# Two waited fills behind every fourth indirect transfer in place of one unwaited fill behind each

## The chip, the cores and the metric

The kernel runs on one core of a Trainium2 chip. A core has five engines that run side by side: TensorE (PE in the profile), VectorE (DVE), ScalarE (ACT), GpSimd (POOL) and SyncE (SP). They meet at semaphores. The metric is the device time of one execution in microseconds. The kernel before took 2920.82 us, the median of three runs from 2917.95 to 2922.92 us.

## What is computed

Two layers of a network on a graph of 3125 nodes with 256 features, and 50,000 edges. Each layer adds a sum over edges, an attention term and the output of experts, with a normalisation between the parts.

```python
# layer 0: messages over edges
support = x @ weight
out = segment_sum(support[col] * edge_weight[:, None], row) + bias
# layer 0: eight private experts, two chosen per node, and a shared one
routed = sum(gate[e] * (gelu(x @ W1p[e] + b1p[e]) @ W2p[e] + b2p[e])); out = shared + routed
# layer 1: messages over edges, weighted by exp(score) per head
messages = h_fwd[src] * direction[:, 0:1] + h_rev[src] * direction[:, 1:2]
# layer 1: a graph-attention router over 32768 edges picks two of four experts
```

Everything that is read or written by an index (rows of edges, of nodes, of experts' slots) goes through indirect transfers.

## The kernel before

Nodes stand in 25 tiles of 128 rows. Edges are first put in the order of their target: each of the 391 columns of 128 edge records is scattered to its place in a table in HBM. Then a stage reads the sorted table back, gathers the source row of each edge (128 rows a transfer), and TensorE sums 128 edges into a tile of nodes by a product with a one-hot matrix that VectorE makes.

All indirect transfers are issued by GpSimd, from one list of instructions in program order:

- `scatter_records` (L840): 391 columns of layer 0's edges (`slots_gnn<-rec_gnn`), later 391 of layer 1's in two parts of 48 and 343.
- `gather_rows` (L1232): 416 gathers of `support` rows for `sum0_stage`. A ring of 16 tiles (`FLIGHT`) is refilled, and before every fourth gather (`HALF` is 4) GpSimd waits for `used`, which TensorE sets when a half of eight tiles has been multiplied.
- `send_nodes0` (L1700): 50 scatters of normed rows to the experts' slots; `fetch_outputs0` (L1721): 50 gathers of the experts' output.
- `gather_messages` (L2373): 440 gathers for layer 1's sum (`sum1_stage`).
- `norm3_table_g_stage` (L2707): 25 scatters; `attend_stage` (L2947, L2959): 256 gathers of `table_g` rows in eleven cuts of about 24, each behind a wait for VectorE, then 25 gathers.

That makes 391 + 416 + 48 + 50 + 343 + 50 + 440 + 25 + 256 + 25 = 2044 indirect transfers. In the scatters and in `gather_messages` GpSimd waits before every fourth transfer until the four that were issued sixteen earlier have landed.

Behind each of the 2044 transfers the helper `breathe` (L816 to L819) issues a fill of one bf16 element per partition: `pool.memset(c.idle[:, c.breaths:c.breaths + 1], 0.0)`. Nothing reads the element. It signals no semaphore and nobody waits for it. So that no two fills write the same element, `c.idle` is 512 wide (`BREATHS`) and in some stages is laid over other tiles that are not in use (`idle_sum0`, `before`, `head32`); the profile shows it as `idle`, `idle_sum`, `before` or `head` at L818.

Beside the transfers, in the order of the program: norm, attention and sort work of layer 0 runs beside the first scatter; the router and the first three chunks of the shared expert run beside the sends and the second scatter; then the private experts (L1843, L1855) run with GpSimd waiting for their output.

Of the kernel before, what the change touches and what calls it, by code (L numbers as in the profile page):

```python
# [21 lines left out]
BF16 = mybir.dt.bfloat16  # L22
# [5 lines left out]
P = 128  # L28
# [8 lines left out]
HALF = RING // 2  # L37
# [29 lines left out]
class Core:  # L67
# [16 lines left out]
    def clear_spent(self):  # L84

        self.nc.all_engine_barrier()
        self.nc.clear_and_free_semaphores(self.spent)
        self.nc.all_engine_barrier()
        self.spent = []
        self.breaths = 0  # L90


def meet(eng, met, n):
# [15 lines left out]
def stage_setup(c, ctx):  # L109
# [13 lines left out]
    c.part = c.sb(ctx, "part", [P, 1])  # L123
    c.head32 = c.sb(ctx, "head32", [P, P])
    c.head64 = c.sb(ctx, "head64", [P, P])
    c.idle = c.sb(ctx, "idle", [P, BREATHS], BF16)
    c.breaths = 0
    c.rows_loaded = c.sem(ctx, "node_rows_loaded")
    const_sem = c.sem(ctx, "constants_made")
    c.tail_zeroed = c.sem(ctx, "tail_zeroed")  # L130
# [682 lines left out]
        ch.then(dve.tensor_copy(self.e.idx[:], self.bank[:, 0:self.e.per]))  # L813


def breathe(c, pool):  # L816

    pool.memset(c.idle[:, c.breaths:c.breaths + 1], 0.0)  # L818
    c.breaths += 1  # L819


def scatter_records(c, block, ctx, e, begin=0, end=None):
# [861 lines left out]
PLACED_A_ROUND = 5  # L1684
SHARED_FIRST = 3
SCATTERED_FIRST = 48
BREATHS = 512


def send_nodes0(c, block, ctx):  # L1690
# [1151 lines left out]
def attend_stage(c, block, ctx, er, e1, y, b2, b2_in, met_n):  # L2842
# [91 lines left out]
    @block.gpsimd  # L2934
    def _(pool):
        pool.wait_ge(met, 4 * (met_n - 1))
        pool.sem_inc(turns, 1)
        for k, (lo, hi) in enumerate(cuts):
            if k >= 2:
                pool.wait_ge(taken, k - 1)  # L2940
                pool.sem_inc(turns, 1)
            for j in range(lo, hi):
                h, turn = j % FLIGHT // HALF, j // FLIGHT
                if j % HALF == 0 and turn:
                    pool.wait_ge(rows_in[h], 16 * HALF * turn)
                    pool.sem_inc(turns, 1)
                pool.indirect_dma_start(rows[:, k % 2, j - lo, :], None, c.table_g,  # L2947
                                        bass.IndirectOffsetOnAxis(er.idx[:, j:j + 1], 0)).then_inc(rows_in[h], 16)
                breathe(c, pool)
        for h in range(2):  # L2950
            pool.wait_ge(stored[h], 16 * len(cuts[h::2]))
            pool.sem_inc(turns, 1)
        c.idle, c.breaths = c.before[:].bitcast(BF16), 0
        for t in range(T):
            h, turn = t % RING // HALF, t // RING
            if t % HALF == 0 and turn:
                pool.wait_ge(ends_in[h], 16 * HALF * turn)
                pool.sem_inc(turns, 1)
            pool.indirect_dma_start(at_end[:, t, :], None, er.states,  # L2959
                                    bass.IndirectOffsetOnAxis(er.end_at[:, t:t + 1], 0)).then_inc(ends_in[h], 16)  # L2960
            breathe(c, pool)
# [465 lines left out]
def build(nc, a, out, upto=4):  # L3427


    c = Core(nc, a, out)  # L3430
    c.upto = upto
    with ExitStack() as top:
        top.enter_context(nc.allow_non_contiguous_dma("small strided rows"))
        c.kept.append(top)
        stage_setup(c, top)
        c.support = nc.dram_tensor("support", [NP, D], F32, kind="Internal").ap()

# [6 lines left out]
        with ExitStack() as l0:  # L3444
# [5 lines left out]
            with ExitStack() as s, nc.Block() as block:  # L3450
# [7 lines left out]
                with ExitStack() as st:  # L3458
                    sort_stage(c, block, st, er, 4)
                load_slots(c, block, l0, e0)  # L3460
                kept_idle = c.idle
                c.idle, c.breaths = c.sb(s, "idle_sum0", [P, BREATHS], BF16), 0
                wait_for_clears = clear_slots0(c, block, s, er)
                sum0_stage(c, block, s, e0, Placing(c, s, er, c.bank[:, 7, :]), Ranking(c, s, e1, c.bank[:, 6, :]))
                block.scalar(wait_for_clears)
            c.idle = kept_idle
            c.clear_spent()
        if c.upto >= 2:
            with ExitStack() as l1:
# [31 lines left out]
                if c.upto >= 3:  # L3501
# [9 lines left out]
                    with nc.Block() as block:  # L3511
                        with ExitStack() as s:
# [6 lines left out]
                            for stage in (lambda st, m: sum1_stage(c, block, st, e1, mix, m),  # L3519
                                          lambda st, m: norm3_table_g_stage(c, block, st, er, e1, m)):  # L3520
                                m += 1
                                with ExitStack() as st:
                                    stage(st, m)
                        c.idle, c.breaths = c.head32[:].bitcast(BF16), 0
                        y = c.sb(l1, "experts_out", [P, EXPERTS1 - 1, T, D])
                        b2 = c.sb(l1, "b2_1", [P, EXPERTS1, D])
                        b2_in = c.sem(l1, "b2_loaded_1")
# [57 lines left out]
```

## Time and profile before

| | us |
|---|---|
| median of three runs | 2920.82 |
| lowest and highest | 2917.95, 2922.92 |
| span of the profiled execution | 4223.8 |
| POOL busy in the profiled execution | 2236.3 (53%) |
| PE busy | 2387.8 (57%) |
| DVE busy | 1680.7 (40%) |
| ACT busy | 1177.6 (28%) |

The profile shows one execution, made with the profiler on. Its span is 4223.8 us, and the kernel's own median is 2920.82 us: the profiled execution is longer by 1303 us, a factor of 1.446. A stretch of the profile can therefore not be taken as the same stretch of a timed run. In the rows, "busy" leaves out semaphore and register instructions, and "idle before" is the time that an engine stood still before an instruction, with what ended it; "issue" means that nothing that the profile shows was waited for.

### The profile page before, as it was taken

To read this page: it belongs to the slowest core of one execution; us is meant where nothing else is said; L and a number is where in the kernel's file an instruction comes from. 1 tells how busy PE (TensorE), PEld (TensorE's weight loads), DVE (VectorE), ACT (ScalarE), POOL (GpSimd) and SP (SyncE) were. 2 spreads that over 40 slices of the span, in tenths; PEclk is the share of its full clock that TensorE was granted. 3 is DMA by queue.
4 is the path that set the end of the run, shared out by engine and by line. 5 is a ranking of instruction groups with operands and counts; after the bars stand their busy time and mean duration, and the time that the engine had idled before them with its cause. 6 is when DMAs were issued, how large, how long until landed. Compare 5 with 4: busy or idle time off the path is not lost. (4 is left out here: it accounts for less than half of the span.)

```text
span 4223.8 us, 36587 instructions
## 1 busy us (share of the span) xinstructions
PE 2387.8 (57%) x9996; PEld 1783.9 (42%) x9997; DVE 1680.7 (40%) x4678; ACT 1177.6 (28%) x3151; POOL 2236.3 (53%) x4104
## 2 busy tenths in 40 slices
PE   0034245445555536443259999736776675677784
PEld 0021134323443335112148887624455454455563
DVE  6510049955577731000000001435777674212225
ACT  0000013534444411000012221235785452222232
POOL 5777740057777755777730001367677735445441
PEclk9985555567777756555579999867997785778787
DMA  1000000043333312000036664122222231010101
GB/s 45 2 18 14 14 3 3 1 178 89 91 88 89 87 32 84 2 2 2 2 106 195 195 190 155 56 73 47 44 46 46 48 21 38 8 21 14 21 13 33
DMA packets 173406, 233.47 MB, mean 55 GB/s; under 512 B 59819, under 2 KB 136622, under 8 KB 172206
## 3 DMA queue, kind: packets, MB, share of 16 engines
q0 software_dynamic: 73664, 103.00, 11.2%
q1 hardware_dynamic: 96888, 118.21, 8.9%
q10 hardware_dynamic: 2678, 10.29, 0.6%
q8 instruction: 65, 1.06, 0.1%
q14 instruction: 111, 0.91, 0.1%
HBM read 192.31 MB, written 39.04 MB: 55 GB/s over the span
## 5 line engine op out<-in xcount | busy, mean ns | idle before, releaser
L840 POOL DMA_INDIRECT slots_gnn<-rec_gnn,slot_row_gnn x782 | 754.5, 965 | 299.6 <-issue 237.7
L1232 POOL DMA_INDIRECT rows_gnn<-support,xT x416 | 402.0, 966 | 437.1 <-DMA xT<-slots_gnn 276.9
L2373 POOL DMA_INDIRECT arena<-table,rec_gnn x440 | 443.8, 1009 | 195.2 <-issue 90.8
L2947 POOL DMA_INDIRECT source_rows<-table_g,source_router x256 | 242.0, 945 | 252.5 <-DVE weighted_rows L3191 158.9
L1277 PE MATMUL banks<-rows_gnn,one_hot 128*128 128x256 f32 x832 | 267.9, 483 | 184.1 <-issue 161.9
L3071 PE MATMUL banks<-xT,w 128*128 128x256 f32 (+1 forms) x832 | 232.0, 411 | 159.3 <-issue 148.2
L1721 POOL DMA_INDIRECT expert_row_ring<-slot_y,slot_from x50 | 48.0, 961 | 510.7 <-SPq L1822 457.3
L1277 PEld LDWEIGHTS banks<-rows_gnn,one_hot 128*128 128x128 f32 x832 | 197.2, 248 | 247.0 <-issue 205.6
L2472 PE MATMUL banks<-weighted,one_hot 128*128 128x260 f32 x880 | 273.4, 464 | 37.9 <-issue 22.1
L3071 PEld LDWEIGHTS banks<-xT,w 128*128 128x128 f32 x832 | 169.2, 209 | 210.6 <-issue 178.8
L1843 PE MATMUL banks<-slot_xT,w_private 128*128 128x256 f32 x1024 | 229.6, 383 | 33.5 <-ACT hidden_private L1885 31.5
L2472 PEld LDWEIGHTS banks<-weighted,one_hot 128*128 128x128 f32 x880 | 191.0, 227 | 97.7 <-issue 62.1
L1885 ACT ACTIVATE hidden_private<-banks,b_private 128x256 f32<-128x256 f32 x256 | 107.3, 470 | 447.0 <-PE banks L1843 417.7
L1855 PE MATMUL banks<-w_private,hidden_private 128*128 128x256 f32 x1024 | 226.1, 379 | 0.0
L1843 PEld LDWEIGHTS banks<-slot_xT,w_private 128*128 128x128 f32 x1024 | 196.7, 192 | 61.4 <-ACT hidden_private L1885 31.7
L796 ACT ACTIVATE lane_one_hot<-lanes_apart,packed_router,packed_minus_router 128x128 bf16<-128x128 bf16 x512 | 203.9, 480 | 2.1
L1855 PEld LDWEIGHTS banks<-w_private,hidden_private 128*128 128x128 f32 x1024 | 192.2, 190 | 24.9
L1497 DVE TENSOR_TENSOR shared_out<-banks,b 128x512 f32<-128x512 f32 (+1 forms) x8 | 5.3, 658 | 493.3 <-remote 492.9
L1631 PE MATMUL banks<-w,hidden_shared 128*128 128x256 f32 x240 | 121.0, 566 | 132.6 <-issue 128.4
L1310 DVE TENSOR_TENSOR x<-banks,x 128x256 f32 x416 | 176.0, 423 | 45.6 <-issue 0.8
L3084 PE MATMUL banks<-w,hidden 128*128 128x256 f32 x668 | 174.6, 407 | 27.0 <-issue 26.8
L790 ACT ACTIVATE lanes_apart<-iota,slot_lane_router 128x128 bf16<-128x128 bf16 x256 | 81.2, 388 | 384.6 <-remote 271.8
(562 smaller groups left out, 4667.0 us busy)
## 6 DMA issues: line engine op xcount, KB each, us to landing
w_private<-in_w1p SPq DMA_DIRECT2D x32, 1024.0 KB
w_private<-in_w2p SPq DMA_DIRECT2D x32, 1024.0 KB
slots_gnn<-rec_gnn,slot_row_gnn POOLq DMA_INDIRECT x782
slot_x<-zero_rows ACTq DMA_DIRECT2D x8, 1024.0 KB
slot_rows<-slot_x SPq DMA_DIRECT2D x32, 256.0 KB
slot_y<-slot_out SPq DMA_DIRECT2D x32, 256.0 KB, 2.2
arena<-table,rec_gnn POOLq DMA_INDIRECT x440
rows_gnn<-support,xT POOLq DMA_INDIRECT x416
```

The lines of the kernel that those rows point to most:

```text
L796: op = act.activation(self.lane_hot[:, b % 2, k, q, :], self.apart[:, b % 2, k, :], ACT.Relu, bias=e.value[:, q, j:j + 1], scale=e.minus[: ...
L840: pool.indirect_dma_start(e.slots, bass.IndirectOffsetOnAxis(e.rows[:, j:j + 1], 0), e.rec[:, j, :], None)\
L1232: pool.indirect_dma_start(e.rows_in[:, k, :], None, table, bass.IndirectOffsetOnAxis(row, 0))\
L1277: mm = pe.matmul(bank_of(k // per), hot[:, k, :], e.rows_in[:, row, :], start=k % per == 0, stop=k % per == per - 1)
L1310: dve.tensor_tensor(x, bank_of(g), x, ALU.add).then_inc(added, 1)
L1843: mm = pe.matmul(hidden_room(f), w1[:, b, k, f * P:(f + 1) * P], xT[:, b, k, :], start=k == 0, stop=k == KD - 1)
L1855: mm = pe.matmul(c.bank[:, 6 + b, j * D:(j + 1) * D], hid[:, b, f, j * P:(j + 1) * P], w2[:, b, f, :], start=f == 0, stop=f == FC - 1)
L2373: pool.indirect_dma_start(c.raw[:, t % RAW_RING, :], None, c.table1, bass.IndirectOffsetOnAxis(row, 0))\
L2472: mm = pe.matmul(c.bank[:, k // per, 0:AGG], hot[:, k, :], val[:, k, :, :].rearrange("p h f -> p (h f)"), start=k % per == 0, stop=k % per ...
L2947: pool.indirect_dma_start(rows[:, k % 2, j - lo, :], None, c.table_g, bass.IndirectOffsetOnAxis(er.idx[:, j:j + 1], 0)).then_inc(rows_in[h ...
L3071: mm = pe.matmul(hidden_room(n, f, (hi - lo) * P), w1[:, x % 2, k, f * P:(f + 1) * P], c.xT[:, k, lo * P:hi * P], start=k == 0, stop=k == ...
L3084: mm = pe.matmul(out_room(n, t - lo), hid(n, f)[:, (t - lo) * P:(t - lo + 1) * P], w2[:, x % 2, f, :], start=f == 0, stop=f == FC - 1)
```

## The change

`breathe` no longer fills behind each transfer. It counts, and at every fourth transfer it calls a new helper, `rest`, which fills one element twice. Each fill signals a semaphore, and GpSimd waits for it before it goes on. The counter runs through the whole program and isn't set back. The wide `idle` tile, the tiles laid over it and the constant `BREATHS` go; one element and a semaphore `rested` come.

```diff
--- before.py
+++ after.py
@@ -87,7 +87,6 @@
         self.nc.clear_and_free_semaphores(self.spent)
         self.nc.all_engine_barrier()
         self.spent = []
-        self.breaths = 0
 
 
 def meet(eng, met, n):
@@ -123,8 +122,9 @@
     c.part = c.sb(ctx, "part", [P, 1])
     c.head32 = c.sb(ctx, "head32", [P, P])
     c.head64 = c.sb(ctx, "head64", [P, P])
-    c.idle = c.sb(ctx, "idle", [P, BREATHS], BF16)
-    c.breaths = 0
+    c.idle = c.sb(ctx, "idle", [P, 1], BF16)
+    c.rested = c.sem(ctx, "rested")
+    c.breaths = c.rests = 0
     c.rows_loaded = c.sem(ctx, "node_rows_loaded")
     const_sem = c.sem(ctx, "constants_made")
     c.tail_zeroed = c.sem(ctx, "tail_zeroed")
@@ -813,10 +813,19 @@
         ch.then(dve.tensor_copy(self.e.idx[:], self.bank[:, 0:self.e.per]))
 
 
+def rest(c, pool):
+
+    for _ in range(2):
+        pool.memset(c.idle[:], 0.0).then_inc(c.rested, 1)
+        c.rests += 1
+        pool.wait_ge(c.rested, c.rests)
+
+
 def breathe(c, pool):
 
-    pool.memset(c.idle[:, c.breaths:c.breaths + 1], 0.0)
     c.breaths += 1
+    if c.breaths % HALF == 0:
+        rest(c, pool)
 
 
 def scatter_records(c, block, ctx, e, begin=0, end=None):
@@ -1684,7 +1693,6 @@
 PLACED_A_ROUND = 5
 SHARED_FIRST = 3
 SCATTERED_FIRST = 48
-BREATHS = 512
 
 
 def send_nodes0(c, block, ctx):
@@ -2950,7 +2958,6 @@
         for h in range(2):
             pool.wait_ge(stored[h], 16 * len(cuts[h::2]))
             pool.sem_inc(turns, 1)
-        c.idle, c.breaths = c.before[:].bitcast(BF16), 0
         for t in range(T):
             h, turn = t % RING // HALF, t // RING
             if t % HALF == 0 and turn:
@@ -3458,12 +3465,9 @@
                 with ExitStack() as st:
                     sort_stage(c, block, st, er, 4)
                 load_slots(c, block, l0, e0)
-                kept_idle = c.idle
-                c.idle, c.breaths = c.sb(s, "idle_sum0", [P, BREATHS], BF16), 0
                 wait_for_clears = clear_slots0(c, block, s, er)
                 sum0_stage(c, block, s, e0, Placing(c, s, er, c.bank[:, 7, :]), Ranking(c, s, e1, c.bank[:, 6, :]))
                 block.scalar(wait_for_clears)
-            c.idle = kept_idle
             c.clear_spent()
         if c.upto >= 2:
             with ExitStack() as l1:
@@ -3521,7 +3525,6 @@
                                 m += 1
                                 with ExitStack() as st:
                                     stage(st, m)
-                        c.idle, c.breaths = c.head32[:].bitcast(BF16), 0
                         y = c.sb(l1, "experts_out", [P, EXPERTS1 - 1, T, D])
                         b2 = c.sb(l1, "b2_1", [P, EXPERTS1, D])
                         b2_in = c.sem(l1, "b2_loaded_1")
```

In GpSimd's list this turns 2044 fills without a wait into 1022 fills with one. In the first scatter (L840 before, L849 after), from the transfer that waits for the landing of an earlier four (`records_moved`), before:

```order
L840 DMA slots_gnn0<-rec_gnn0,slot_row_gnn0 53639x4 [waits records_moved_gnn0_0_0]
L818 MEMSET idle 128x1
L840 DMA slots_gnn0<-rec_gnn0,slot_row_gnn0 53639x4
L818 MEMSET idle 128x1
L840 DMA slots_gnn0<-rec_gnn0,slot_row_gnn0 53639x4
L818 MEMSET idle 128x1
L840 DMA slots_gnn0<-rec_gnn0,slot_row_gnn0 53639x4
L818 MEMSET idle 128x1
L840 DMA slots_gnn0<-rec_gnn0,slot_row_gnn0 53639x4 [waits records_moved_gnn0_0_1]
```

and of the change:

```order
L849 DMA slots_gnn0<-rec_gnn0,slot_row_gnn0 53639x4 [waits rested,records_moved_gnn0_0_0]
L849 DMA slots_gnn0<-rec_gnn0,slot_row_gnn0 53639x4 x3
L819 MEMSET idle 128x1
L819 MEMSET idle 128x1 [waits rested]
L849 DMA slots_gnn0<-rec_gnn0,slot_row_gnn0 53639x4 [waits rested,records_moved_gnn0_0_1]
```

Four transfers stand back to back; the second fill waits for the first, and the next transfer for the second.

In the gathers of `sum0_stage` (L1232 before, L1241 after; `rows_used0` is what TensorE sets), before:

```order
L1232 DMA rows_gnn0<-support,xT 128x256 [waits rows_used0]
L818 MEMSET idle_sum0 128x1
L1232 DMA rows_gnn0<-support,xT 128x256
L818 MEMSET idle_sum0 128x1
L1232 DMA rows_gnn0<-support,xT 128x256
L818 MEMSET idle_sum0 128x1
L1232 DMA rows_gnn0<-support,xT 128x256
L818 MEMSET idle_sum0 128x1
L1232 DMA rows_gnn0<-support,xT 128x256 [waits rows_used0]
```

and of the change:

```order
L1241 DMA rows_gnn0<-support,xT 128x256 [waits rows_used0]
L819 MEMSET idle 128x1
L819 MEMSET idle 128x1 [waits rested]
L1241 DMA rows_gnn0<-support,xT 128x256 [waits rested]
L1241 DMA rows_gnn0<-support,xT 128x256 x2
L1241 DMA rows_gnn0<-support,xT 128x256 [waits rows_used0]
```

Since 391 transfers went before, the pair of fills stands here behind the gather that waits for TensorE, and not ahead of it.

## Rows read from the trace of the kernel before

**Rows 1.** The page's head: span, busy time of each engine, its slices.
```profile
span 4223.8 us, 36587 instructions
PE 2387.8 (57%) x9996; PEld 1783.9 (42%) x9997; DVE 1680.7 (40%) x4678; ACT 1177.6 (28%) x3151; POOL 2236.3 (53%) x4104
POOL 5777740057777755777730001367677735445441
```

**Rows 2.** Busy us (and instructions) of each engine in stretches; then clock, DMA share, GB/s.
```profile
core 0: us, PE busy (x) PEld busy (x) DVE busy (x) ACT busy (x) POOL busy (x), PEclk, DMA share, GB/s
38.00:594.00 556.00, 139.81 (x320) 74.11 (x321) 155.84 (x431) 28.21 (x44) 425.08 (x782) 0.76 0.05 10
594.00:870.00 276.00, 134.66 (x1464) 108.67 (x1463) 234.55 (x437) 95.01 (x194) 0.00 (x0) 0.53 0.02 6
870.00:1488.00 618.00, 332.33 (x1316) 245.08 (x1317) 401.36 (x1229) 282.02 (x768) 456.71 (x832) 0.77 0.35 105
1488.00:1684.00 196.00, 100.28 (x402) 82.73 (x401) 54.99 (x200) 22.38 (x49) 105.88 (x196) 0.63 0.19 59
1684.00:2168.00 484.00, 175.62 (x324) 88.68 (x324) 8.53 (x13) 16.74 (x42) 368.16 (x686) 0.51 0.04 8
2168.00:2624.00 456.00, 450.24 (x2136) 395.90 (x2136) 43.57 (x63) 104.75 (x250) 0.00 (x0) 0.99 0.58 182
...
2759.00:3424.00 665.00, 425.12 (x1426) 287.27 (x1427) 424.25 (x1111) 372.32 (x1174) 494.64 (x880) 0.80 0.26 49
...
3553.00:4078.00 525.00, 362.67 (x1399) 284.55 (x1401) 104.75 (x433) 120.44 (x246) 271.59 (x512) 0.78 0.11 18
```

**Rows 3.** Timeline of POOL in the first scatter: start us, us, instruction, idle before.
```profile
48.41 0.98 POOL L840 DMA_INDIRECT slots_gnn<-rec_gnn,slot_row_gnn  x1 [0.19 <-issue]
49.39 0.12 POOL L818 MEMSET idle<- 128x1 bf16 x1
49.69 0.96 POOL L840 DMA_INDIRECT slots_gnn<-rec_gnn,slot_row_gnn  x1 [0.19 <-issue]
50.65 0.12 POOL L818 MEMSET idle<- 128x1 bf16 x1
50.95 0.96 POOL L840 DMA_INDIRECT slots_gnn<-rec_gnn,slot_row_gnn  x1 [0.19 <-issue]
```

**Rows 4.** POOL's groups over the span: count | busy us, mean ns | idle before, releasers.
```profile
L1232 POOL DMA_INDIRECT rows_gnn<-support,xT x416 | 402.0, 966 | 437.1 <-DMA xT<-slots_gnn 276.9 <-remote 80.0 <-issue 60.0
L2373 POOL DMA_INDIRECT arena<-table,rec_gnn x440 | 443.8, 1009 | 195.2 <-issue 90.8 <-DMA support<-support_ring 41.1 <-PE banks L2472 35.2
L2947 POOL DMA_INDIRECT source_rows<-table_g,source_router x256 | 242.0, 945 | 252.5 <-DVE weighted_rows L3191 158.9 <-issue 93.4
L1721 POOL DMA_INDIRECT expert_row_ring<-slot_y,slot_from x50 | 48.0, 961 | 510.7 <-SPq L1822 457.3 <-DVE x L2120 46.1 <-issue 7.3
```

**Rows 5.** Timeline of POOL in the setup: an instruction that waits for POOL's own fill.
```profile
1.36 0.20 POOL L143 MEMSET ident<- 128x128 f32 x1
1.81 0.28 POOL L144 TENSOR_SCALAR_AFFINE_SELECT ident<-ident 128x128 f32<-128x128 f32 x1 [0.24 <-POOL ident L143]
```

**Rows 6.** Timeline where POOL stood in a wait: in `sum0_stage`, then in `attend_stage`.
```profile
999.65 1.11 DVE L1298 TENSOR_SCALAR one_hot<-iota,xT 128x128 f32<-128x128 f32 x4 [3.65 <-PE banks L1277]
1000.40 0.94 POOL L1232 DMA_INDIRECT rows_gnn<-support,xT  x1 [2.21 <-PE banks L1277]
...
3708.14 0.90 DVE L3191 TENSOR_TENSOR weighted_rows<-source_rows,edge_weights 128x384 f32<-128x384 f32 x1 [40.26 <-ACT edge_weights L2998]
...
3710.23 0.94 POOL L2947 DMA_INDIRECT source_rows<-table_g,source_router  x1 [20.04 <-issue]
```

**Rows 7.** Waits in the stretch 1684 to 2168 us: total us, times, longest.
```profile
DVE shared_out L1497 <- remote: 458.9, 6, 89.6
...
PEld banks L1631 <- issue: 157.9, 137, 2.6
...
PE banks L1618 <- issue: 111.9, 104, 2.4
POOL slots_gnn L840 <- issue: 109.5, 343, 2.2
PE banks L1631 <- issue: 109.0, 106, 2.2
```

## The prediction

> **What bounds the kernel now.** I read the page's head first. No engine is busy for more than 57% of the span, so the end is set by different engines in different stages; the slices of POOL show GpSimd at 7 to 8 tenths in four long stretches, broken by stretches of zero [rows 1]. The table of stretches says what each is [rows 2]. From 38 to 594 us (the first scatter), 870 to 1488 us (the gathers of `sum0_stage`), 1684 to 2168 us (the second scatter) and 2759 to 3424 us (the gathers of `sum1_stage`) POOL is busy for 74 to 76% of the time, and no other engine is above 65%. From 2168 to 2624 us PE is busy for 450 of 456 us, and POOL for none. From 3553 to 4078 us PE leads with 363 of 525.
>
> Why POOL is at 75% and still the bound shows in its timeline [rows 3]. A transfer takes 0.96 us, the fill starts where it ends and takes 0.12 us, and the next transfer starts 0.19 us after the fill, "issue" being all that it waited for. The period from start to start is 1.26 us (49.69 to 50.95), and the 0.19 us count as idle. So GpSimd has no free time in such a stretch. Where it really waits, its groups tell [rows 4]: 80 us for "remote" work in the gathers of `sum0_stage`, 41 + 35 us in those of `sum1_stage`, 159 us for VectorE in the table gathers of `attend_stage`, 46 us for VectorE in the fetches behind the experts (the 457 us before them are one wait for the experts' output).
>
> **What is removed.** The count is exact: 2044 fills without a wait. For four transfers the time between the end of one and the start of the next is 4 x (0.12 + 0.19) = 1.24 us now [rows 3].
>
> **What is added.** 511 times (2044 / 4) a pair of fills, each waited for. Take the time between transfers for a group of four after the change. Between the four transfers there are three gaps without a fill. The trace has no two transfers back to back, so the gap is bounded by 0 (the 0.19 us belong to the fill) and 0.19 us (they belong to the transfer). I take 0.19 us: it is the same before each transfer in the steady rows, and the fill itself starts with no gap at all, so the gap goes with the kind of instruction that follows. Then comes the first fill, 0.12 us. The second fill waits for the first: the nearest row is the setup's L144, which waits for POOL's own fill L143; that ends at 1.36 + 0.20 = 1.56 us and L144 starts at 1.81, 0.24 us later [rows 5]. The second fill takes another 0.12 us. Then the next transfer waits for it, and this is the term that matters. Before the change GpSimd's sequencer has the next transfer ready behind the fill; after it, the transfer can only be begun once the semaphore is there. What that costs shows where POOL stood in a wait [rows 6]. At 999.65 us VectorE and at 1000.40 us GpSimd start behind the same TensorE product: GpSimd's transfer is 0.75 us later. In `attend_stage` VectorE's product that frees the buffer ends at 3708.14 + 0.90 = 3709.04 us, and the transfer starts at 3710.23, 1.19 us later. The bounds for a restart are thus 0.24 us (if a transfer restarts as fast as L144) and 1.19 us; I take 0.75, since one semaphore alone is waited for, as at 1000.40.
>
> The group: 3 x 0.19 + 0.12 + 0.24 + 0.12 + 0.75 = 1.80 us in place of 1.24, so **+0.56 us for four transfers**, 11% of 5.04 us. With 1.19 us it is +1.00, with 0.24 us +0.05, and with the lower bound of both (0 and 0.24) -0.52 us.
>
> A rule of the notes speaks against the 0.75 us. The Trainium skill, "DMA: Bandwidth & Descriptors", section "Anatomy of one DMA — SWDGE (gpsimd) path", puts the dispatch by the sequencer at about 50 ns and the generation of descriptors at "small, variable". By it the restart would be an estimated 0.05 + 0.19 = 0.24 us and the group +0.05 us, the second rival below. The trace's 0.75 us [rows 6] does not agree with it, and the trace decides.
>
> **What queues behind the waits.** Everything behind a fill on GpSimd is the next transfer; for it wait TensorE's products in the two sums (they need the gathered rows) and, in the scatters, the reload of the sorted table, which needs all of them. By stages, in the profiled execution's time:
>
> - first scatter, 391 transfers, 98 groups: 98 x 0.56 = 55 us.
> - gathers of `sum0_stage`, 416, 104 groups: 58 us. The 80 us in which GpSimd waits for others [rows 4] can take some: what POOL loses between two such waits shortens the next. I count half, 29 us.
> - 48 scatters and 50 sends ahead of the experts, 24 groups: 14 us.
> - second scatter, 343, 86 groups: 48 us.
> - gathers of `sum1_stage`, 440, 110 groups: 62 us against 76 us of waits; half, 31 us.
> - the 25 scatters and 25 gathers at the router's ends, 12 groups: 7 us.
> - `attend_stage`'s 256 gathers (64 groups, 36 us) are hidden by its 159 us of waits for VectorE, the 50 fetches (12 groups, 7 us) by their 46 us [rows 4]. Without that cover they would cost 43 us.
>
> Sum: 55 + 29 + 14 + 48 + 31 + 7 = **184 us** of a span of 4224 us, 4.4%. The smaller `idle` tile moves no work.
>
> **From the profiled execution to the timed one.** The span is 1.446 times the median of 2920.82 us, and the trace doesn't say where the 1303 us lie. PE's stretch at 450 of 456 us cannot have lost much, so the GpSimd stretches must have. A first way is to scale: 184 / 1.446 = 127 us, which gives 3048. But in the two scatters GpSimd isn't alone in being slow. TensorE issues 324 products in 484 us there, against 2136 in 456 us in the next stretch, and between them it stands in gaps of "issue", 112 + 109 us [rows 2, 7]. Much of that is work that in a faster execution would end earlier or later than the scatter by itself, and behind the first scatter VectorE is busy for 235 of 276 us. I can't tell from the trace whether GpSimd is still the bound in the two scatters when the kernel is timed, and count half of their 103 us. That leaves 184 - 52 = 132 us, and 132 / 1.446 = **91 us: 3012 us**, 3.1% slower.
>
> **Rivals.**
>
> 1. *The restart is dearer* (1.19 us, +1.00 for a group). The row at 3710.23 speaks for it; the one at 1000.40 is closer to the case. 91 x 1.00 / 0.56 = 163 us gives 3084; with the scatters in full, 127 x 1.79 = 227 us gives 3148. It would also hold if back-to-back transfers were slower each than those with a fill between, of which the trace shows nothing.
>
> 2. *The wait is cheap or covered.* A restart at L144's 0.24 us makes +0.05 us for a group: 434 groups on the path x 0.05 / 1.446 = 15 us, 2936. If in the timed execution VectorE, TensorE and ScalarE are the bound in both sums (they are busy for 401 of 618 and 425 of 665 us already, with a POOL that is slow), next to nothing is left, and the time stays at 2921. For it: those busy shares. Against: a scatter of 98 transfers ahead of the experts and the ends of the router have no cover.
>
> 3. *It gets faster*: the 0.19 us belong to the change from a fill to a transfer. Then three of four gaps go, and the group is 0.12 + 0.24 + 0.12 + restart. It is a gain as soon as the restart is under 1.24 - 0.48 = 0.76 us; at 0.75 it is nothing, at 0.50 it is -0.26 us, and 434 x 0.26 / 1.446 = 78 us less gives 2843. In the same direction: if TensorE's "issue" gaps in the scatters [rows 7] come from GpSimd's transfers, each pause behind a fourth transfer lets TensorE go on. Against: the fill starts behind a transfer without any gap, so no gap goes with a change of kind as such.
>
> That the change doesn't do what it says is excluded by GpSimd's order: four transfers, two fills, the waits on `rested`.
>
> **How the numbers follow.** The forecast (a restart near 0.75 us, partly covered) has 0.62, and spans 2950 to 3125. Rival 1 beyond 3125 has 0.08, rival 2 has 0.17 (0.10 of it within 0.2% of 2920.82, which is about what a measurement of this kernel can tell from no change, and 0.07 slower by 2927 to 2950), rival 3 has 0.13. The likeliest is the forecast, 3012 us. The range must leave out no more than 0.2: at the upper end it cuts at 3125 and leaves out 0.08; at the lower end it takes in rival 2 whole and ends at 2915, leaving out nearly all of rival 3. Faster 0.13, same 0.10, slower 0.62 + 0.08 + 0.07 = 0.77.
>
> **What would show it.** In the changed kernel's profile, in the first scatter: three gaps of 0.19 us between transfers of 0.96 us, then two fills of 0.12 us with 0.24 us between, and 0.75 us to the next transfer; 5.6 us from the first transfer of a group to that of the next, where it is 5.05 now. A gap of 0 between transfers is rival 3, a restart of 0.24 us rival 2, one of 1.2 us rival 1. The span should be near 4224 + 184 = 4408 us; the waits for others in the gathers of both sums shorter than 80 and 76 us; the stretch of the private experts unchanged at some 456 us. The forecast is wrong if the timed execution isn't bound by GpSimd where the profiled one is, or if a transfer's own duration depends on what stands before it.

## The result: 5.1% slower, and a profile of before from another condition

| | us |
|---|---|
| kernel before, median of four runs beside it | 2919.39 (2917.41 to 2922.92) |
| change, median of four runs | 3070.11 (3061.61 to 3071.31) |
| ratio | 1.0507, 95% interval 1.0495 to 1.052 |
| span of the change's profile | 3068.5 |

The change is 151 us slower; the prediction had said 91. The head of its page:

```profile
span 3068.5 us, 35567 instructions
PE 2195.5 (72%) x9997; PEld 1686.8 (55%) x9997; DVE 1684.1 (55%) x4678; ACT 1184.5 (39%) x3151; POOL 2134.3 (70%) x3082
...
POOL 4667676667777776777777754777777772777761
```

The span is no longer than the timed run. The profile of before had 4223.8 us [rows 1], so by the two profiles the change would be 27% faster, and by the timed runs it is 5.1% slower. The two profiles can't be compared: one and the same program, the kernel before, took 2919 and 2925 us in two sessions (below: *quick*) and 4178, 4185 and 4222 us in three others (below: *slow*), each time with little spread. The profile of before belongs to the second kind, and profiling is not what makes it long, as the first experiment shows. The three slow sessions ran on three different chips (numbers 7, 6 and 4) and the second quick one on a fourth (number 0); for the first quick one and the profile of before the chip isn't on record. No chip was used twice, so nothing here tells whether a chip is slow or a time is.

The first scatter in the change, GpSimd's timeline (start us, us, instruction, idle before):

```profile
55.59 0.96 POOL L849 DMA_INDIRECT slots_gnn<-rec_gnn,slot_row_gnn  x1 [0.30 <-issue]
56.85 0.95 POOL L849 DMA_INDIRECT slots_gnn<-rec_gnn,slot_row_gnn  x1 [0.30 <-issue]
58.11 1.01 POOL L849 DMA_INDIRECT slots_gnn<-rec_gnn,slot_row_gnn  x1 [0.30 <-issue]
59.12 0.27 POOL L819 MEMSET idle<- 128x1 bf16 x2
60.21 0.96 POOL L849 DMA_INDIRECT slots_gnn<-rec_gnn,slot_row_gnn  x1 [0.82 <-POOL idle L819]
```

Two things stand here that the rows of before could not show. Between two transfers with no fill there are 0.30 us, exactly the 0.12 + 0.19 us that stood there with one [rows 3]: from start to start it is 1.26 us with and without. And behind the pair of fills it takes 0.82 us until a transfer that has a landing's wait ahead of it too. Where no such wait follows, it is 0.28 us. In the program, that place holds two things between the pair and the transfer: the wait for the landing, and an increment of the semaphore `turns` by GpSimd itself. No run separates the two. Without a waited fill ahead of them they cost nothing: in the kernel with no fill at all (below), the longest gap of this kind before a scatter is 0.3 us too. So "directly ahead of the landing's wait" means below: ahead of the wait and its increment.

### The profile page after: what moved, and what is told of

It is laid out like the page before. It is cut to its first block and busy times, and to the rows that moved or that the text cites. A ratio compares the mean times of both kernels' runs of the same rounds, so it can differ in the third digit from the quotient of the medians.

```text
span 3068.5 us, 35567 instructions
## 1 busy us (share of the span) xinstructions
PE 2195.5 (72%) x9997; PEld 1686.8 (55%) x9997; DVE 1684.1 (55%) x4678; ACT 1184.5 (39%) x3151; POOL 2134.3 (70%) x3082
## 5 line engine op out<-in xcount | busy, mean ns | idle before, releaser
L849 POOL DMA_INDIRECT slots_gnn<-rec_gnn,slot_row_gnn x782 | 767.4, 981 | 341.5 <-issue 189.5
L2381 POOL DMA_INDIRECT arena<-table,rec_gnn x440 | 454.9, 1034 | 157.3 <-issue 100.4
L1286 PE MATMUL banks<-rows_gnn,one_hot 128*128 128x256 f32 x832 | 320.0, 497 | 294.4 <-DMA rows_gnn<-support,xT 279.2
L1241 POOL DMA_INDIRECT rows_gnn<-support,xT x416 | 402.4, 967 | 132.0 <-issue 98.1
L1286 PEld LDWEIGHTS banks<-rows_gnn,one_hot 128*128 128x128 f32 x832 | 164.3, 233 | 427.8 <-DMA rows_gnn<-support,xT 219.3
L1307 DVE TENSOR_SCALAR one_hot<-iota,xT 128x128 f32<-128x128 f32 x416 | 118.4, 356 | 220.1 <-DMA xT<-slots_gnn 120.9
L2480 PEld LDWEIGHTS banks<-weighted,one_hot 128*128 128x128 f32 x880 | 193.1, 229 | 63.0 <-issue 26.1
L3078 PE MATMUL banks<-xT,w 128*128 128x256 f32 (+1 forms) x832 | 183.7, 375 | 7.5 <-DMA w<-in_w2e 7.5
L2451 ACT ACTIVATE weighted<-arena,edge_weight 128x65 f32<-128x65 f32 x660 | 169.3, 335 | 3.5 <-PE banks L2480 1.7
L3078 PEld LDWEIGHTS banks<-xT,w 128*128 128x128 f32 x832 | 155.1, 192 | 28.3 <-DMA w<-in_w2e 7.6
L3091 PE MATMUL banks<-w,hidden 128*128 128x256 f32 x668 | 158.5, 385 | 10.8 <-ACT xT L3022 10.8
L2429 ACT ACTIVATE arena<-arena,rec_gnn 128x68 f32<-128x68 f32 x440 | 112.4, 337 | 133.5 <-DMA arena<-table,rec_gnn 133.5
```

The lines of the kernel that those rows point to most:

```text
L849: pool.indirect_dma_start(e.slots, bass.IndirectOffsetOnAxis(e.rows[:, j:j + 1], 0), e.rec[:, j, :], None)\
L1241: pool.indirect_dma_start(e.rows_in[:, k, :], None, table, bass.IndirectOffsetOnAxis(row, 0))\
L1286: mm = pe.matmul(bank_of(k // per), hot[:, k, :], e.rows_in[:, row, :], start=k % per == 0, stop=k % per == per - 1)
L2381: pool.indirect_dma_start(c.raw[:, t % RAW_RING, :], None, c.table1, bass.IndirectOffsetOnAxis(row, 0))\
L2451: op = act.activation(val[:, k, hd, :], m, ACT.Copy, scale=prob[:, i % 2, k, hd:hd + 1])
L2480: mm = pe.matmul(c.bank[:, k // per, 0:AGG], hot[:, k, :], val[:, k, :, :].rearrange("p h f -> p (h f)"), start=k % per == 0, stop=k % per ...
```

## Experiments

All kernels compute everything, since fills write only an element that nothing reads.

### The kernel before again

No edit.

> The kernel before, unchanged, profiled once more. Its first profile spans 4223.8 us at a median of 2919 us, and in it TensorE has gaps of 0.7 to 2.2 us that nothing explains while small rows are moved. If the stretch belongs to this kernel's profile (many fills and transfers in a row on GpSimd), the span is near 4224 again. If it was one disturbed execution, the span is near 2920.

Measured: 4181.36 us timed in that very run, span 4179.6; the kernel before beside it 4177.76 us (nine runs, 4170.94 to 4196.32). So neither a single disturbed execution nor the profiler: the whole session was slow. Its profile repeats that of before. TensorE in the second scatter; these products wait for nothing that the profile shows:

```profile
1799.73 1.01 PE L1618 MATMUL banks<-xT,w 128*128 128x256 f32 x2 [0.91 <-issue]
1801.85 1.31 PE L1618 MATMUL banks<-xT,w 128*128 128x256 f32 x2 [1.11 <-issue]
1804.67 1.28 PE L1618 MATMUL banks<-xT,w 128*128 128x256 f32 x2 [1.51 <-issue]
```

### No fill at all

```diff
 def breathe(c, pool):
-    pool.memset(c.idle[:, c.breaths:c.breaths + 1], 0.0)
     c.breaths += 1
```

It ran in three sessions. The first two were slow:

> No fill at all behind any transfer. Theory A (a fill that nobody waits for stands inside a gap of 0.305 us that is there between two transfers anyway, and costs nothing; the change's price is all in the waits): 2919 us, within 5. Theory B (the unwaited fills are what makes the kernel before quick: without one between them, transfers take longer in a timed run): 3000 us or more. Theory C (a fill costs its 0.12 us): 2044 x 0.12 us on a path for the most part, 2750 us.

Measured: 4249.95 us against 4177.76, ratio 1.0174, interval 1.0146 to 1.0201.

> No fill at all, once more, beside the kernel before. Where the kernel before takes 2919 us: theory A (an unwaited fill is free) says 2919 within 5 us, theory B (it makes transfers quicker) 3000 or more, theory C (it costs 0.12 us) 2750. Where it takes 4180 us: 4250 again.

Measured: 4288.23 us against 4222.2, ratio 1.0158, interval 1.013 to 1.0186.

> No fill at all, a third time. Where the kernel before takes 2919 us: theory A (an unwaited fill is free) 2919 within 5 us, theory B (it makes transfers quicker) 3000 or more, theory C (it costs 0.12 us) 2750. Where it takes about 4200 us: some 1.6% more than the kernel before, as twice already.

Measured, in a quick session: **2919.87 us against 2924.67, ratio 0.9994, interval 0.9984 to 1.0004**. Theory A holds: 2044 unwaited fills cost nothing and bring nothing. All of the change's 5.1% lies in its pairs of waited fills; that it is the waits and not the fills, the timeline of the next experiment shows. In a slow session the same unwaited fills do bring something. With none between the transfers TensorE's gaps are 2.21 us each:

```profile
1799.89 0.59 PE L1617 MATMUL banks<-xT,w 128*128 128x256 f32 x1 [2.21 <-issue]
1801.29 0.29 PEld L1617 LDWEIGHTS banks<-xT,w 128*128 128x128 f32 x1 [2.51 <-issue]
1802.69 0.59 PE L1617 MATMUL banks<-xT,w 128*128 128x256 f32 x1 [2.21 <-issue]
1804.09 0.29 PEld L1617 LDWEIGHTS banks<-xT,w 128*128 128x128 f32 x1 [2.51 <-issue]
1805.49 0.59 PE L1617 MATMUL banks<-xT,w 128*128 128x256 f32 x1 [2.21 <-issue]
```

Weight loads (PEld) and products take turns, and each starts 1.40 us after the other: TensorE gets one instruction off in 1.40 us, of whichever kind. From 1750 to 2150 us it is 143 loads and 144 products in 400 us, again 1.40 us for each.

Since this kernel takes the time of the kernel before in a quick session, its profile from that session (span 2917.0 us) can stand for the profile of before that was missing. Stretches of it, cut at GpSimd's stages (the same columns as [rows 2]):

```profile
38.00:552.10 514.10, 223.34 (x1784) 170.64 (x1784) 386.56 (x867) 123.17 (x238) 395.17 (x391) 0.69 0.10 29
...
558.40:1085.70 527.30, 371.20 (x1330) 219.01 (x1330) 408.43 (x1251) 284.04 (x768) 400.84 (x416) 0.84 0.36 106
1085.70:1227.90 142.20, 128.02 (x586) 111.61 (x586) 52.27 (x184) 34.53 (x77) 94.32 (x99) 0.83 0.28 83
1227.90:1661.10 433.20, 427.05 (x2042) 375.44 (x2041) 43.74 (x64) 100.03 (x241) 328.85 (x343) 0.99 0.64 186
1661.10:1711.50 50.40, 47.14 (x223) 41.16 (x221) 4.15 (x6) 9.73 (x24) 0.01 (x1) 1.00 0.38 121
...
1813.60:2404.20 590.60, 447.55 (x1567) 303.84 (x1567) 466.32 (x1220) 402.21 (x1290) 456.78 (x440) 0.87 0.28 56
...
2490.30:2813.60 323.30, 320.59 (x1494) 280.74 (x1496) 109.85 (x454) 135.28 (x269) 245.54 (x256) 0.99 0.16 31
```

The same stages in the change:

```profile
38.00:630.50 592.50, 224.04 (x1784) 170.36 (x1784) 384.53 (x867) 123.23 (x238) 414.29 (x585) 0.66 0.09 25
...
636.90:1196.40 559.50, 393.98 (x1331) 228.87 (x1332) 411.61 (x1254) 284.13 (x768) 427.81 (x624) 0.80 0.35 100
1196.40:1345.20 148.80, 133.40 (x635) 117.63 (x634) 53.19 (x183) 37.02 (x85) 101.08 (x149) 0.85 0.26 78
1345.20:1804.50 459.30, 453.42 (x2152) 398.25 (x2151) 45.08 (x66) 106.80 (x256) 347.14 (x513) 0.99 0.63 188
1804.50:1821.10 16.60, 13.39 (x63) 11.44 (x61) 1.38 (x2) 0.45 (x2) 0.27 (x3) 1.00 0.11 36
...
1923.30:2538.60 615.30, 456.13 (x1567) 311.19 (x1567) 470.30 (x1224) 404.87 (x1297) 478.78 (x660) 0.85 0.27 53
...
2625.30:2964.70 339.40, 330.90 (x1535) 289.07 (x1534) 109.88 (x454) 134.14 (x269) 257.19 (x384) 0.98 0.15 28
```

| stage | no fill | change | difference |
|---|---|---|---|
| first scatter, 391 | 514.1 | 592.5 | +78.4 |
| gathers of `sum0_stage`, 416 | 527.3 | 559.5 | +32.2 |
| 48 scatters, 50 sends | 142.2 | 148.8 | +6.6 |
| second scatter, 343 | 433.2 | 459.3 | +26.1 |
| wait for the experts behind it | 50.4 | 16.6 | -33.8 |
| gathers of `sum1_stage`, 440 | 590.6 | 615.3 | +24.7 |
| table gathers, 256 | 323.3 | 339.4 | +16.1 |
| all else | 335.9 | 337.1 | +1.2 |
| span | 2917.0 | 3068.5 | +151.5 |

The first scatter alone has half of the loss. The second scatter's 26 us are taken out of GpSimd's wait for the experts, in which TensorE is at 99% of the full clock and busy: from 1085.7 to 1711.5 us it is 626 us, in the change from 1196.4 to 1821.1 it is 625.

### Two fills at every fourth transfer, unwaited

```diff
 def breathe(c, pool):
-    pool.memset(c.idle[:, c.breaths:c.breaths + 1], 0.0)
     c.breaths += 1
+    if c.breaths % HALF == 0:
+        pool.memset(c.idle[:, c.breaths - 2:c.breaths - 1], 0.0)
+        pool.memset(c.idle[:, c.breaths - 1:c.breaths], 0.0)
```

> At every fourth transfer two fills of different elements, with no semaphore and no wait: the change without its waits. Theory A: the first fill is hidden in the gap, the second may add its 0.12 us to 511 gaps, so 2919 to 2970 us. Theory B (pacing by a fill behind each transfer matters): like the change, 3050 to 3070 us. The profile should show transfer, two fills, transfer with 0.43 us between transfers if the second fill isn't hidden.

Measured, in the first slow session: 4238.33 us against 4177.76, ratio 1.0138 (1.0106 to 1.017), close to no fill at all. The time can't test theory A there, and this kernel wasn't timed in a quick session, but the timeline can:

```profile
52.24 0.96 POOL L842 DMA_INDIRECT slots_gnn<-rec_gnn,slot_row_gnn  x1 [0.30 <-issue]
53.20 0.12 POOL L820 MEMSET idle<- 128x1 bf16 x1
53.23 0.12 POOL L821 MEMSET idle<- 128x1 bf16 x1
53.51 0.96 POOL L842 DMA_INDIRECT slots_gnn<-rec_gnn,slot_row_gnn  x1 [0.16 <-issue]
```

The second fill starts 0.03 us after the first, and the next transfer 0.31 us after the end of the last. Even two unwaited fills fit into the gap.

### One waited fill in place of two

```diff
 def rest(c, pool):
-    for _ in range(2):
+    for _ in range(1):
```

> One waited fill at every fourth transfer in place of two. Theory A: a group's gap is 0.12 + 0.28 = 0.40 us against 0.56 with two and 0.305 with none, where no other wait stands behind it; where the wait for a landing stands right behind it (98 groups of the first scatter, 12 of the fetches) the loss is nearly as large as with two, some 0.6 us. Together 98 x 0.6 + 400 x 0.09 = 95 us less cover: 2990 us, between 2970 and 3020. Theory B: as the change, 3070 us.

Measured, in the same slow session: 3919.65 us against 4177.76, ratio 0.9394 (0.9359 to 0.9428). The expectation was for a quick session and isn't tested. What came instead was the first sign that a wait behind the transfers is a gain in a slow one. Where it lies shows in the first scatter, in GpSimd's timeline, and in the stretches of the first and the second scatter (the columns of [rows 2]):

```profile
58.48 0.12 POOL L819 MEMSET idle<- 128x1 bf16 x1
59.42 0.96 POOL L849 DMA_INDIRECT slots_gnn<-rec_gnn,slot_row_gnn  x1 [0.82 <-issue]
...
38.00:617.00 579.00, 236.13 (x1784) 174.29 (x1784) 383.18 (x866) 125.56 (x238) 405.60 (x488) 0.67 0.05 10
1422.60:1902.40 479.80, 126.34 (x211) 60.70 (x212) 4.15 (x6) 11.73 (x28) 338.64 (x428) 0.50 0.02 2
```

One fill ahead of the landing's wait makes a pause of 0.12 + 0.82 = 0.94 us, and in the first scatter TensorE does all of its 1784 products. In the second scatter, where the same fill stands away from the wait (0.12 + 0.28 = 0.40 us), it does 211.

### The change again

> The changed kernel once more, beside the kernel before. In the last session the kernel before took 4178 us and not 2919, with TensorE standing in gaps of 0.7 to 2.2 us while GpSimd moves small rows; with one waited fill 3920, with none 4250. Theory S (there is a condition of the chip in which a GpSimd queue that is full of transfers holds TensorE up, and draining it twice at every fourth transfer ends that): where the kernel before takes 4178 us, the change takes near 3070, as in its first profile. Theory T (the whole session was slow, whatever the kernel): the change takes some 4300 us where the kernel before takes 4178. Where the kernel before takes 2919 us, both say 3070.

Measured, in a second slow session: 3886.77 us against 4185.1, **ratio 0.928 (0.926 to 0.930)**. The sign is turned round: 5.1% slower in a quick session, 7.2% faster in a slow one. Theory S was too good (it had 3070), theory T is out. Where the gain lies, in the stretches of the first scatter and of the second:

```profile
38.00:627.00 589.00, 231.37 (x1784) 171.72 (x1784) 383.75 (x867) 125.22 (x238) 410.41 (x585) 0.66 0.09 25
...
1435.00:1914.00 479.00, 146.66 (x257) 72.91 (x257) 5.53 (x8) 12.56 (x32) 346.47 (x513) 0.50 0.02 2
```

In the first scatter TensorE does its 1784 products, and the gathers begin at 633.5 us. In the profile of before it did 320 by 594 us, 1464 came behind the scatter, and the gathers began at 870 [rows 2]. In the second scatter it is held up as before.

### The pairs away from the landing's wait

```diff
-    if c.breaths % HALF == 0:
+    if c.breaths % HALF == 2:
         rest(c, pool)
```

> The change with its pairs of fills moved by two transfers, so that in the first scatter (98 pairs) and the fetches (12) none stands directly ahead of the wait for a landing; nothing else differs. In the profile of the change a pair costs 0.79 us there (2.05 in place of 1.26 us from transfer to transfer) and 0.25 us elsewhere. Theory A (the two waits in a row add up): 110 x 0.54 = 59 us less than the change, 3011 us where that takes 3070; at least the first scatter is shorter by 98 x 0.54 = 53 us. Rival (the wait for the landing itself ends later, whatever stands before it): the same as the change.

Measured, in the same slow session: 4110.07 us against 4185.1, ratio 0.9816 (0.9793 to 0.9839), so 223 us more than the change, where 59 less had been expected. In GpSimd's list of the first scatter the expectation holds: a pair costs 0.28 us of fills and 0.28 us of gap, 0.56 in place of 0.30. But the first scatter's gain is gone; TensorE has 272 products by 587 us:

```profile
38.00:587.00 549.00, 136.32 (x272) 66.07 (x272) 138.78 (x412) 25.38 (x43) 405.47 (x587) 0.68 0.05 10
587.00:872.00 285.00, 144.94 (x1514) 119.09 (x1513) 244.44 (x457) 97.95 (x195) 0.00 (x0) 0.53 0.02 6
```

The gathers begin at 872 us, and in the change at 633.5. The same number of fills and waits stands in both; what differs is where, and with it the length of the pause. That gave two theories for the next two kernels.

"Nothing else differs" was not right, though. The counter runs through the whole program, so the move by two also brings the pairs of `sum1_stage`, which stood away from the landing's wait, directly ahead of it:

```profile
3000.16 0.27 POOL L819 MEMSET idle<- 128x1 bf16 x2
3001.35 0.94 POOL L2381 DMA_INDIRECT arena<-table,rec_gnn  x1 [0.91 <-issue]
```

That stage takes 700 us here and 655 in the change's profile of the same session. And the 12 pairs of the fetches did not get away from a wait, since once their ring is full these wait before each transfer. The name "away from the wait" holds for the two scatters, and the reading on TensorE rests on them alone.

### The pairs on the wait everywhere; six fills away from it

The first sets the counter back at the head of each list of transfers:

```diff
         pool.wait_ge(e.filled, 16)
+        c.breaths = 0
         for j in range(begin, end):
```

(and so on in the gathers of both sums, the sends, the fetches, the table gathers and the last gathers).

> The change with its counter set back at the start of each list of transfers, so that a pair of fills stands directly ahead of every wait for a landing or for a used half, as in the first scatter of the change; also between the 256 table gathers. Each such pair costs 0.79 us where the other wait is long over, against 0.25 us off the wait. Where the kernel before takes about 2919 us, the second scatter's 86, the sums' 214 and the table gathers' 64 pairs get dearer by up to 0.54 us: up to 190 us over the change, 3150 to 3260 us. Where the kernel before takes about 4180 us: in the change, the first scatter (pairs on the wait) left TensorE without gaps and the second (pairs off the wait) did not. Theory P (the long pause of 1.1 us with the queue drained is what frees TensorE): no gaps in the second scatter either, 3500 to 3750 us against the change's 3887. Theory Q (the first scatter's relief has another cause): 3890 us or more.

Measured, in a third slow session: 3553.32 us against 4222.2, ratio 0.842 (0.8391 to 0.8449), inside theory P's range. The gaps in the second scatter did not go altogether, as theory P had it; its stretch:

```profile
1432.00:1936.00 504.00, 419.65 (x1668) 322.01 (x1669) 35.47 (x52) 82.05 (x200) 347.35 (x513) 0.91 0.38 114
```

1668 products, where the change in a slow session had 257 in its second scatter, and in a quick one 2152.

The second takes the kernel with the pairs away from the wait and makes them longer:

```diff
 def rest(c, pool):
-    for _ in range(2):
+    for _ in range(6):
...
-    if c.breaths % HALF == 0:
+    if c.breaths % HALF == 2:
         rest(c, pool)
```

> The pairs of fills two transfers away from the landing's wait, but six waited fills each time and not two. Each more waited fill adds 0.16 us (0.057 us gap and 0.10 us), so a group pauses 0.25 + 4 x 0.16 = 0.89 us longer than without fills, as long as one pair on the wait (0.79). Where the kernel before takes 2919: 3011 + 511 x 0.64 us less cover, 3200 to 3330 us. Where it takes 4180: by theory P (the pause's length frees TensorE) its gaps in the scatters are gone and the first scatter ends with the sort stage done, 3700 to 3900 us; by the rival (it is the landing's wait right behind the fills, with nothing queued beyond it) TensorE still stands in gaps, 4100 us or more.

Measured, in the same session: **3434.07 us against 4222.2, ratio 0.8129 (0.8108 to 0.8151)**. It is below the 3700 to 3900 us that theory P had. It differs from the kernel with 4110 us in the number of fills alone. GpSimd now stands for 0.92 us in fills and 0.28 in a gap, and in the first and the second scatter TensorE is not held up:

```profile
52.49 0.92 POOL L819 MEMSET idle<- 128x1 bf16 x6
53.69 0.96 POOL L849 DMA_INDIRECT slots_gnn<-rec_gnn,slot_row_gnn  x1 [0.28 <-POOL idle L819]
```

The stretches of the same kernel's first and second scatter (the columns of [rows 2]):

```profile
38.00:644.00 606.00, 232.06 (x1784) 171.63 (x1784) 384.73 (x867) 124.69 (x238) 461.50 (x979) 0.66 0.09 25
...
1443.00:1955.00 512.00, 466.40 (x2048) 371.37 (x2049) 41.51 (x60) 100.41 (x242) 381.06 (x859) 0.99 0.54 163
```

2048 products in the second scatter, where the kernel before had 324 [rows 2]. Theory P is borne out: the pause between transfers frees TensorE, and its length decides, 1.20 us at every fourth transfer nearly in full, 0.56 us hardly. The number of fills doesn't: one fill with a pause of 0.94 us freed TensorE in the first scatter, two with 0.56 us did not. The rival, that the landing's wait is what does it, is out, since in the two scatters none stands here directly behind the fills. Every long pause was made of waits, though; whether a pause of the same length in which GpSimd works without waiting does the same was not run.

### Six fills, but only where rows are small

Out of the kernel with six fills, `breathe` is taken from `gather_rows`, `gather_messages` and `fetch_outputs0`.

> Six waited fills at every fourth transfer, away from the landing's wait, but only in the scatters and the gathers of small rows; none in the gathers of both sums and the fetches, where TensorE showed no gaps in any profile. Where the kernel before takes about 4200 us: the relief of TensorE stays and the pauses in the sums go, which took 631 and 777 us with six fills against 605 and 648 with one or none: 3434 - 155 = 3280 us. If the pauses in the sums had relieved something too, it stays at 3434. Where the kernel before takes 2919: the pauses of the scatters and the small gathers alone, up to 253 us, 3080 to 3170.

Measured, in the second quick session: 3132.23 us against 2924.67, ratio 1.0714 (1.0696 to 1.0732), inside the 3080 to 3170 that was expected for it. Whether it is the better kernel in a slow session isn't known.

### The change without fills in the first scatter

```diff
+                c.quiet = True
                 scatter_records(c, block, s, e0)
...
-    if c.breaths % HALF == 0:
+    if c.breaths % HALF == 0 and not c.quiet:
```

(`c.quiet` is set to False behind that block's list.)

> The change, but without fills in the first scatter (391 transfers); all else as in the change. Where the kernel before takes 2919 us: if GpSimd sets the end of that stage, 98 x 0.79 = 77 us less than the change, 2993; if another engine does, 3070. Where it takes about 4200 us: in the change TensorE has no gaps in the first scatter and the gathers start at 633 us and not at 870. Theory P (the pauses free TensorE) says that this goes and comes back as a loss of some 235 us: 4120 us. If the earlier start had another cause, 3887 less 77 us, 3810.

Measured, in the same quick session: 2989.40 us against 2924.67, ratio 1.023 (1.0209 to 1.0251), 81 us under the change's 3070.11, where 77 had been expected. In its profile the first scatter takes 514.6 us, as with no fill at all (514.1). So in a quick session GpSimd sets the end of the first scatter's stage, in full and with no cover.

### All runs

| kernel | session | us | ratio to before |
|---|---|---|---|
| before | quick | 2919.39, 2924.67 | 1 |
| before | slow | 4177.76, 4185.10, 4222.20 | 1 |
| change | quick | 3070.11 | 1.0507 |
| no fill | quick | 2919.87 | 0.9994 |
| change, first scatter without | quick | 2989.40 | 1.0230 |
| six fills, small rows alone | quick | 3132.23 | 1.0714 |
| no fill | slow | 4249.95, 4288.23 | 1.0174, 1.0158 |
| two unwaited fills at the fourth | slow | 4238.33 | 1.0138 |
| pairs away from the wait in the scatters | slow | 4110.07 | 0.9816 |
| one waited fill | slow | 3919.65 | 0.9394 |
| change | slow | 3886.77 | 0.9280 |
| pairs on the wait everywhere | slow | 3553.32 | 0.8420 |
| six fills away from the wait in the scatters | slow | 3434.07 | 0.8129 |

No version is quicker than the kernel before in a quick session (without fills it is the same); in the slow one the last two beat it by 16 and 19%, the change by 7%.

## The prediction, step by step

**The direction and the place were right, the size was not.** It said 3012 us, and 3070 was measured, inside its range of 2915 to 3125. The price does lie in restarts of GpSimd's list, and mostly where it has no cover. But that 91 and 151 us lie as near as this is in part luck, since errors of both signs stand in the sum. After its halvings and its division by 1.446, the prediction had 19 us for the first scatter (measured 78.4), 20 and 21 for the two sums (32.2 and 24.7), 26 for the transfers ahead of the experts with the second scatter (measured with the wait behind it: -1.1) and nothing for the table gathers (16.1).

**The step "from the profiled execution to the timed one" failed.** It took the 1303 us for something spread over GpSimd's stretches and divided by 1.446. The profile came from a slow session. A transfer has the same median of 1.26 us from start to start in both, so nothing of the sum should have been divided. What differs is mostly TensorE, whose gaps the prediction saw in rows 7 but didn't name as the reason: of the 825 us between the change's own two profiles (3893.3 and 3068.5 us), GpSimd's wait for the experts' output, 480.7 against 16.3 us, has 464. Halving the first scatter on top of it was the worst single step: 55 us was halved and divided to 19, and 78.4 were measured; that GpSimd sets the end of this stage, which the halving doubted, the change without fills in it shows. With its shares of cover and its price of 0.56 us undivided, the sum would have been 184 us, nearer to the 151 than its 91.

**The price of a group was wrong in both directions.** It was put at +0.56 us everywhere. Measured: +0.25 us where no other wait follows (0.28 of fills and 0.28 of gap, against 0.305), and +0.79 us where the landing's wait follows (the median from start to start is 2.05 in place of 1.26 us; 58.11 to 60.21 in the rows above). The terms: the gap between transfers without a fill, put at 0.19 us, is 0.30 us, which lies outside the stated bounds of 0 and 0.19. The rows could not show that the fill stood inside a gap that is there anyway; no fill at all showed it. The wait of the second fill for the first, put at 0.24, is 0.06 us: the pair takes 0.27 to 0.28 us, one fill 0.12, and the second one 0.10. The restart, put at 0.75, is 0.28 us, and 0.82 where a wait with its increment stands ahead of it. The row at 1000.40 was such a place: the program has a wait and an increment of `turns` before that transfer, so it was the nearest row for about a fifth of the groups only. From group to group in the first scatter, 5.6 us were forecast, and 3 x 1.26 + 2.05 = 5.8 us came; the span of 4408 us that was forecast for the profile came in neither kind of session (3068.5 and 3893.3 us).

**The rule of the Trainium skill** ("DMA: Bandwidth & Descriptors", "Anatomy of one DMA — SWDGE (gpsimd) path") would have put the restart at an estimated 0.24 us. The measured 0.28 us agrees with it where the fill's wait stands alone; the 0.82 us does not. That the trace's 0.75 us decided against it was right for about one group in five (the first scatter's 98 and the fetches' 12, of 511) and wrong for the rest.

**Cover.** `sum0_stage`: 58 us halved to 29, and 32 measured; `sum1_stage`: 62 halved to 31, 25 measured; both near by two errors that cancel, a price of 0.56 in place of 0.25 us and a cover of half where there was next to none: the measured price of the groups is 104 x 0.25 = 26 and 110 x 0.25 = 28 us. The second scatter: 48 us on the path, and with the 14 us of the transfers ahead of it none measured (626 us against 625 from those transfers to the end of GpSimd's wait), since in a quick session the experts run beside it and GpSimd waits for them. The table gathers: 0 on the path, 16 measured (64 x 0.25); their 159 us of waits for VectorE belong to the slow session, in the quick one 0.3 us are left.

**The rivals.** The third, that it gets faster since a pause lets TensorE go on, is what happens in a slow session, by 7.2%; it had 0.13. Its other half, that the gap of 0.19 us goes when no fill is there, is wrong: the gap is 0.30 us then. The second has the restart right away from the landing's wait (0.24 us, 0.28 measured), but not the price (+0.05 us a group, +0.25 measured), and next to nothing was covered in the sums. The first has the nearest time (3084 us) and the wrong reason: a restart of 1.19 us came nowhere.

## What to carry to other kernels

Behind an indirect transfer on GpSimd a fill that nobody waits for was free. A pair of waited ones cost 0.25 us, and 0.79 us directly ahead of another wait and its increment: where the engine's list sets the time, place such pauses away from waits, or not at all. Before a profile is used for a forecast, compare its span with the timed runs. Here a span of 1.446 times the median came from another condition than the timed runs, and most of its waits belonged to that condition. A change that only makes one engine pause should be timed in both conditions before it is called a loss or a gain.

## What was not expected of the hardware

- The same program took 2919 and 2925 us in two sessions and 4178 to 4222 us in three others. In the slow ones TensorE stands still between instructions that wait for nothing while GpSimd issues transfers of small rows. With no fills it starts a load or a product once in 1.40 us; with one fill behind each transfer the gaps in the rows above are 0.9 to 1.5 us; with a pause of 1.2 us behind every fourth they are next to gone. The other engines hardly show it: in the slow profile with no fill, 293 of TensorE's 7595 products that carry no wait start after a gap of 0.5 to 3 us, and of ScalarE's 1846 such instructions none, of VectorE's 1477 only 28.
- The gathers of both sums, with rows of 1 KB and more, are slower in a slow session too, if less: in the change 610 and 655 us, against 559.5 and 615 in the quick one. Their products follow one another closely within a group, but before the groups TensorE stands in more and longer "issue" gaps (total us, times, longest), in `sum0_stage` of the change, slow and then quick:

```profile
PE banks L1286 <- issue: 212.3, 68, 10.1
...
PE banks L1286 <- issue: 10.1, 6, 2.4
```

- What resource TensorE is held up by, and why only in some sessions, stays open; the runs show that pauses of GpSimd relieve it, not through what.
- A fill of one element per partition takes 0.12 us in the timeline and adds nothing to the period of 1.26 us between transfers; two unwaited ones in a row start 0.03 us apart.
- A waited fill that follows a waited fill costs 0.16 us: 0.06 us of wait and 0.10 us of fill (six take 0.92 us).
